# Eight result and twelve token row buffers, eight more slots for late weights, and merges one piece by partition, four tiles later

## The reference, cut to what matters

```
u  = layernorm twice of x;  xz = u @ in_proj.T;  x_in, z = split(xz)          # 256 + 256 features
xc = silu(causal depthwise conv of x_in, 4 taps)
dt, B, C = split(xc @ x_proj.T)                                               # 8, 16, 16
delta = softplus(dt @ dt_w.T + dt_b)
h_t = exp(delta * A) * h_{t-1} + delta * B * xc      # a scan over time, for 256 features x 16 states
y = (sum over states of h * C + xc * D) * silu(z);   x1 = ... + y @ out_w.T
x2 = x1 + (silu(gate) * val) @ ffp.T                  # gate, val from a norm of x1
x3 = x + x2
logits = layernorm(x3) @ Ws + bs;  the two best of 8 experts, weights by softmax
out = x3 + sum over the two experts of weight * (silu(m @ Wg[e]) * (m @ Wu[e])) @ Wd[e]   # 128 -> 344 -> 128
```

## Time and profile before

| what | value |
|---|---|
| median of 3 runs | 918.84 us (916.27 to 920.73) |
| the profiled execution's own time | 916.48 us |
| its span, first to last instruction | 914.6 us |
| mean granted TensorE clock | 0.789 |
| busy: PE, DVE, ACT, POOL | 634.4, 766.2, 447.8, 577.8 us |
| DMA | 126.06 MB, mean 138 GB/s |

### The profile page before, as it was taken

How to read it: one execution, slowest core, us unless ns; L and a number is a source line. 1 busy time by engine, 2 the same in 40 slices (tenths; PEclk the granted TensorE clock), 3 DMA queues, 4 the chain that set the end, 5 groups by cost and what they waited for, 6 DMA issues and landing times.

```text
span 914.6 us, 12461 instructions
## 1 busy us (share of the span) xinstructions
PE 634.4 (69%) x3482; PEld 488.9 (53%) x3482; DVE 766.2 (84%) x1158; ACT 447.8 (49%) x924; POOL 577.8 (63%) x488
## 2 busy tenths in 40 slices
PE   4357377478757785797589658865884686887874
PEld 1134354365346435684477337743773475777863
DVE  1389899999989989989999999999999996363453
ACT  2446455644654475545555564647553352333421
POOL 1096376458746995789668976898589845235422
PEclk9577578758656966997699768977796679799987
DMA  6734233333323346533553355335543553446694
GB/s 175 244 104 142 91 116 100 120 94 121 124 76 96 118 117 169 161 113 99 175 161 107 96 185 151 127 93 161 172 120 113 149 145 94 125 140 191 185 308 132
DMA packets 99767, 126.06 MB, mean 138 GB/s; under 512 B 11831, under 2 KB 63875, under 8 KB 99683
## 3 DMA queue, kind: packets, MB, share of 16 engines
q1 hardware_dynamic: 95155, 115.89, 42.7%
q0 software_dynamic: 4544, 9.38, 2.8%
HBM read 113.23 MB, written 16.34 MB: 142 GB/s over the span
## 4 chain that ended last, share of the span: by engine, by line
DVE 35%; PE 29%; issue 18%; ACT 7%; DMA 4%; SPq 3%; POOL 3%; DVEq 1%; another core or an unknown queue 0%; POOLq 0%; ACTq 0%
DVE state L908 19%; DVE product L916 4%; PE work_front L1062 4%; PE y L1104 3%; PE gate L1181 3%; PE work_front L1068 3%; PE up L1188 3%; PE up L1199 2%; DVE stats L841 2%; PE work_front L1076 1%; DVE silu_m L1027 1%; PE work_side L1142 1%; DMA y_dram<-y_rows,x_rows 1%; DVE x_tok L945 1%; DVE conv L882 1%
## 5 line engine op out<-in xcount | busy, mean ns | idle before, releaser
L670 POOL TENSOR_TENSOR inflow<-du,b_wide 128x1024 f32<-128x1024 f32 x128 | 308.9, 2416 | 191.6 <-DVE product L916 153.8
L775 ACT ACTIVATE decay<-delta,a_neg 128x512 f32<-128x512 f32 x256 | 174.0, 689 | 199.4 <-DVE state L908 191.5
L1104 PE MATMUL y<-ident,product 128*128 128x128 f32 x1024 | 181.8, 337 | 119.9 <-DVE product L916 119.9
L1104 PEld LDWEIGHTS y<-ident,product 128*128 128x128 f32 x1024 | 153.5, 177 | 172.9 <-DVE product L916 138.3
L908 DVE TENSOR_TENSOR_SCAN state<-decay,carry,inflow 128x512 f32<-128x512 f32 x192 | 235.2, 1266 | 0.8 <-ACT decay L775 0.8
L916 DVE TENSOR_TENSOR product<-state,c_wide 128x1024 f32<-128x1024 f32 x128 | 189.5, 1480 | 1.3
L697 POOL DMA_INDIRECT y_dram<-y_rows,x_rows x78 | 87.5, 1121 | 90.5 <-ACT y_rows L831 82.4
L691 POOL DMA_INDIRECT row_dram<-m_tok,place x64 | 71.8, 1122 | 22.1 <-issue 12.8
L908 DVE TENSOR_TENSOR_SCAN state<-decay,inflow 128x512 f32<-128x512 f32 x64 | 74.5, 1205 | 7.0 <-ACT decay L775 4.5
L1062 PE MATMUL work_front<-u_t,w_tap 128*128 128x512 f32 x128 | 63.0, 618 | 4.0 <-ACT u_t L725 1.7
L1181 PE MATMUL gate<-x_cols,w_stage 128*128 128x128 f32 x306 | 50.5, 309 | 7.4 <-ACT x_cols L821 6.9
(11 more groups left out here) (199 smaller groups left out, 1118.4 us busy)
## 6 DMA issues: line engine op xcount, KB each, us to landing
b_wide<-bc_dram SPq DMA_DIRECT2D x128, 256.0 KB
c_wide<-bc_dram SPq DMA_DIRECT2D x128, 256.0 KB
w_stage<-gate_up_dram SPq DMA_DIRECT2D x78, 344.0 KB
x_rows<-row_dram SPq DMA_DIRECT2D x78, 65.0 KB
x_tok<-in_x SPq DMA_DIRECT2D x8, 256.0 KB, 6.0
out<-x_tok SPq DMA_DIRECT2D x8, 256.0 KB
inflow<-y_dram SPq DMA_DIRECT2D x6, 256.0 KB, 4.8
gate_up_dram<-in_Wg SPq DMA_DIRECT2D x1, 1376.0 KB, 9.1
```

The source lines that it names most:

```text
L670: e.tensor_tensor(inflow[:, key % 3], du[:, c % 2], b_wide[:, key % ROW_SLOTS:key % ROW_SLOTS + 1, :].to_broadcast([P, HALVES, CHUNK]), AL ...
L775: e.activation(decay_bank[h][:], delta[:, c % 2, h, :], ACT.Exp, scale=a_neg[:, h, n:n + 1]).then_inc(S["decay"], 1)
L1104: t = e.matmul(y_bank[s // 2][:, y_at(s, h)], product[:, key % 2, h, s * P:(s + 1) * P], ident[:], is_transpose=True, start=False, stop=n ...
```

## The change

- `X_SLOTS` goes from 8 to 12, `Y_SLOTS` from 4 to 8. The wait of `load_x` (L620) is not edited: for a job from 12 on it waits on the semaphore of slot `key % 8` for `(key - 12) // 8 + 1` landings.
- Behind the scan, weights also go to eight more slots, in `xc`, `silu_z`, `delta`, `conv` and `tanh_c`. A load takes the first free slot; `load_w` has its own loop ahead of the row loads, over the next 13 jobs in the tail. The first load into such a slot waits for the last `y_gate`.
- The numbers in `tag` and the view `y_chunks` change, so that a partition's results of a chunk (two experts, four tokens) lie in one run of 4 KB; `fetch_y` is one DMA of 512 KB.
- Fetches of chunks 0 to 6 stand at steps 0, 1, 3, 4, 6, 7 and 9 behind the first; a merge comes four steps behind its fetch, a store five.
- Semaphores: the merge waits on the chunk's `d_x`, four start semaphores become one.

```
-X_SLOTS = 8
-Y_SLOTS = 4
+LATE_SLOTS = 8
+X_SLOTS = 12
+Y_SLOTS = 8
...
+    def load_w(m):
+
+        if m < len(JOBS) and JOBS[m][0] in listed and ("load_w", m) not in done:
+            for q in range(W_SLOTS + (LATE_SLOTS if late else 0)):
+                users = [t for t, (slot, _, _) in w_slot.items() if slot == q]
+                if not users or ("up", users[-1]) in done:
+                    w_slot[m] = q, len(users), users[-1] if users else None
+                    put("load_w", m)
+                    return
...
-            if (m < W_SLOTS or ("up", m - W_SLOTS) in done) and JOBS[m][0] in listed and ("load_w", m) not in done:
-                put("load_w", m)
+            load_w(m)
...
-                for at in range(len(span) + 3):
-                    merges.append([(step, span[at - lag]) for step, lag in (("fetch_y", 0), ("merge", 2), ("store", 3)) if 0 <= at - lag < len(span)])
+                at = {c: k + k // 2 for k, c in enumerate(span)}
+                for now in range(at[span[-1]] + MERGE_LAG + 2):
+                    merges.append([(step, c) for step, lag in (("fetch_y", 0), ("merge", MERGE_LAG), ("store", MERGE_LAG + 1)) for c in span if at[c] + lag == now])
...
+    late.append(last)
     for t in range(m, len(JOBS) + 2):
...
+        for q in range(t, t + W_SLOTS + LATE_SLOTS):
+            load_w(q)
         for q in range(t, t + X_SLOTS):
             load(q, 0)
...
-        y_chunks = y_dram[0:TOPK * TOKENS, :].rearrange("(q c s p) d -> c p q s d", q=TOPK, s=SUB, p=P)
+        y_chunks = y_dram[0:TOPK * TOKENS, :].rearrange("(c p q s) d -> c p q s d", q=TOPK, s=SUB, p=P)
...
-                    for q in range(TOPK):
-                        e.dma_start(y_back[key][:, q], y_chunks[key][:, q]).then_inc(S[f"d_merge{key}"], 16)
+                    e.dma_start(y_back[key], y_chunks[key]).then_inc(S[f"d_x{key}"], 16)
...
-                    if key >= W_SLOTS:
-                        e.wait_ge(S["up"], key - W_SLOTS + 1)
+                    if ahead is not None:
+                        e.wait_ge(S["up"], ahead + 1)
+                    elif q >= W_SLOTS:
+                        e.wait_ge(S["y_gate"], 2 * CHUNKS)
```

More of the change, by code:

```diff
@@ L121 @@
 BACK_BEFORE_ROUND = 6
+MERGE_LAG = 4
 def plan():
@@ L178, in first_half @@
             put("up", m)
-    sent, listed, loaded = set(), set(), {}
+    sent, listed, loaded, w_slot, late = set(), set(), {}, {}, []
     def queue_back(c):
@@ L313, in plan @@
         put(step, last)
-    return order, tail
+    return order, tail, w_slot
 def mamba_moe_block(nc, T, out):
@@ L417, in mamba_moe_block @@
                   for part in (inflow[:, 0], inflow[:, 1], inflow[:, 2], product[:, 0], product[:, 1], state[:, 0], state[:, 1], du[:, 0])]
+        late_parts = [xc[:, 0], xc[:, 1], silu_z[:, 0], silu_z[:, 1], delta[:, 0], delta[:, 1], conv, tanh_c]
+        late_parts = [part.rearrange("p h t -> p (h t)")[:, 0:2 * FF_WIDE].rearrange("p (j f) -> p j f", j=2) for part in late_parts]
+        w_slots = [w_stage[:, q] for q in range(W_SLOTS)] + late_parts
         var_one = sb("var_one", [P, SUB])
@@ L431, in mamba_moe_block @@
         gate_bank, up_bank = bank("gate"), bank("up")
-        order, tail = plan()
+        order, tail, w_slot = plan()
         banks = [(gate_bank, up_bank), tuple(decay_bank), tuple(y_bank)]
@@ L439, in mamba_moe_block @@
             + [f"d_b{q}" for q in range(ROW_SLOTS)] + [f"d_c{q}" for q in range(ROW_SLOTS)]
-            + [f"d_rows{q}" for q in range(X_SLOTS)] + [f"d_w{q}" for q in range(W_SLOTS)] + [f"d_scatter{c}" for c in range(CHUNKS)]
-            + ["d_gate_up", "d_pads", "bases", "tag0", "tag1", "list", "listed_count", "merged"] + [f"d_y{q}" for q in range(Y_SLOTS)] + [f"d_merge{c}" for c in range(CHUNKS)]
-            + ["halved", "a_exp", "a_neg", "diag", "minus_half", "ones", "ser_shift", "w_tap", "back_halved", "halo"]
+            + [f"d_rows{q}" for q in range(X_SLOTS)] + [f"d_w{q}" for q in range(W_SLOTS + LATE_SLOTS)] + [f"d_scatter{c}" for c in range(CHUNKS)]
+            + ["d_gate_up", "d_pads", "bases", "tag0", "tag1", "list", "listed_count", "merged"] + [f"d_y{q}" for q in range(Y_SLOTS)]
+            + ["halved", "a_exp", "a_neg", "diag", "constants", "w_tap", "back_halved", "halo"]
             + ["stats0", "aggr0", "stats2", "aggr2", "stats3", "aggr3", "rstd0", "rstd2", "rstd3", "shift0", "shift2", "shift3"]
@@ L449, in mamba_moe_block @@
             + ["rank", "count", "place"]
-            + ["x_turn", "x_cols", "w_pad", "gate", "up", "tanh_m", "silu_m", "moe_h", "down", "y_rows"])}
+            + ["x_turn", "x_cols", "gate", "up", "tanh_m", "silu_m", "moe_h", "down", "y_rows"])}
         x_dram = T["x"].rearrange("b (c s p) d -> (b c) p s d", s=SUB, p=P)
@@ L597, in _ @@
                     k, j = JOBS[key]
-                    q = key % W_SLOTS
+                    q, use, ahead = w_slot[key]
                     if j == 0:
@@ L626, in _ @@
         def _(e):
-            e.memset(minus_half[:], -0.5).then_inc(S["minus_half"], 1)
-            e.memset(ser_shift[:], LOG1P_SHIFT).then_inc(S["ser_shift"], 1)
-            e.memset(ones[:], 1.0).then_inc(S["ones"], 1)
-            e.memset(w_stage[:, :, :, FF:], 0.0).then_inc(S["w_pad"], 1)
+            e.memset(minus_half[:], -0.5).then_inc(S["constants"], 1)
+            e.memset(ser_shift[:], LOG1P_SHIFT).then_inc(S["constants"], 1)
+            e.memset(ones[:], 1.0).then_inc(S["constants"], 1)
+            e.memset(w_stage[:, :, :, FF:], 0.0).then_inc(S["constants"], 1)
             e.memset(left[:, :, 0:4], 0.0).then_inc(S["bases"], 1)
@@ L1016, in _ @@
                 elif name == "merge":
-                    e.wait_ge(S[f"d_merge{key}"], 16 * TOPK)
+                    e.wait_ge(S[f"d_x{key}"], 16 * 2)
                     for q in range(TOPK):
@@ L1176, in _ @@
                     e.wait_ge(S["x_cols"], key + 1)
-                    e.wait_ge(S[f"d_w{key % W_SLOTS}"], 16 * (key // W_SLOTS + 1))
+                    slot, use, _ = w_slot[key]
+                    e.wait_ge(S[f"d_w{slot}"], 16 * (use + 1))
                     if key == 0:
-                        e.wait_ge(S["w_pad"], 1)
+                        e.wait_ge(S["constants"], 4)
                     for q in range(NF):
-                        t = e.matmul(gate[:, q * P:(q + 1) * P], w_stage[:, key % W_SLOTS, 0, q * P:(q + 1) * P], x_cols[:, key % 2, :], start=True, stop=True)
+                        t = e.matmul(gate[:, q * P:(q + 1) * P], w_slots[slot][:, 0, q * P:(q + 1) * P], x_cols[:, key % 2, :], start=True, stop=True)
                     t.then_inc(S["gate"], 1)
@@ L1187, in _ @@
                     for q in range(NF):
-                        t = e.matmul(up[:, q * P:(q + 1) * P], w_stage[:, key % W_SLOTS, 1, q * P:(q + 1) * P], x_cols[:, key % 2, :], start=True, stop=True)
+                        t = e.matmul(up[:, q * P:(q + 1) * P], w_slots[w_slot[key][0]][:, 1, q * P:(q + 1) * P], x_cols[:, key % 2, :], start=True, stop=True)
                     t.then_inc(S["up"], 1)
```

10 lines of the change are left out of this document (5 added, 5 removed).

## The result

The changed kernel took 925.64 us (median of 20 runs, 918.67 to 931.91); the kernel before, measured beside it, 918.23 us (20 runs, 914.34 to 922.30). The ratio is 1.0074, interval [1.0052, 1.0096]: slower by 0.7%. I had forecast 914.0 us and given "slower" a chance of 0.11. Two later measurements on other chips, each beside runs of the kernel before, gave 0.9998 [0.9969, 1.0027] and 1.0033 [0.9996, 1.0069]. So the sign is settled in one direction only: in no measurement is the change faster, and it costs 0 to 0.7% by the chip or the session. The expected 4.7 us are missing everywhere, and that is the question here.

The account below looks back on a forecast made before the run. DVE was taken to bound the scan; in the tail PE, then merges with DMA share 0.97 and about 12 us of waits. +3.5 - 0.8 - 6.0 - 1.4 = -4.7 us, 914.1 on the median; forecast 914.0, range 905 to 921.

Parts of the forecast that it names:

- The scan: Scan stage: extra row buffers and slot rule change no place in the list, DVE hides semaphore waits; 0, ±1 us.
- Result buffers: Result buffers 4 to 8: ScalarE's long waits are late signals from PE and stay; 0, lower bound -8.3 us.
- The rival that gave 906: Result buffers did bind, so eight remove the four stalls and fetches perhaps come in time: -13 us, 906; chance 0.17.
- Row buffers: Row buffers 8 to 12: rows up to job 59 go ahead of round 7's pads, -0.8 us; a loss in the merges.
- the exact wait: Rival without waits for adds 68 and 69: fetch 1 sooner, fetch 0 not; 0.4 us, inside the range, no own chance.
- The start of round 6: Tail, step 38: ten weight loads ahead of row load 41 delay job 42; +3.5 us, ends +2 and +5.5.
- the second figure: Start of round 6: rows stand behind 3.52 MB of weights in flight, landing at 782.4, +4.6 us; without that, +2.9.
- The merges: Merge stretch: merge 0 waits 5.6 us, merge 1 0.4, later fetches in time; -6.0 us, good end -12.
- the bad end of the range: Merge stretch: landings of 5 us each push fetch 0 and fetch 1, about 899; with a further clock drop 0.
- The end: Behind job 77: adds no longer queue, -1.0; last fetch one issue, -0.4; together -1.4 us, ends -2.4 and 0.
- The gain of the merges is given back: SP's blocked row loads delay fetches 0 and 1, merges give -2, clock's saving fails: 0, 919; chance 0.24.
- The slower rival: Round 6: rows of jobs 41 and 42 behind 3.52 MB, drain about 22 us or more; about 927; chance 0.09.

Follow-up runs that it names:

- e6_slotrule: The kernel before with only the changed kernel's slot rule, the lowest-numbered free weight slot: 919.73 us, ratio 0.9977.
- e9_y8: The kernel before with eight result buffers instead of four, nothing else: 921.43 us, ratio 1.0024.
- e11_y4: The changed kernel with four result buffers instead of eight: 918.15 us, ratio 0.9989 to the kernel before.
- before_again: The kernel before, unchanged, profiled once more on the chip of the others: 917.84 us, ratio 1.0018.
- e3_exact: The changed kernel with each row load waiting for the add twelve jobs back: 911.01 us, ratio 0.9933 to the kernel before.
- e2_oldest: The changed kernel with weight loads taking the slot free for longest, not the lowest-numbered: 917.37 us, ratio 0.9985 to the kernel before.
- e4_rowsfirst: The changed kernel with row loads ahead of the loop of weight loads in each tail step: 917.78 us, ratio 1.0002 to the kernel before.
- x_all: The changed kernel with longest-free slot, row wait for the add twelve jobs back, rows ahead of weights: 900.8 us, 0.9820; on a third chip 902.23 us, 0.9828.
- x_lowest: x_all with the lowest-numbered free weight slot again: 906.38 us, ratio 0.9867 to the kernel before.
- x_y4: x_all with four result buffers instead of eight: 906.29 us, ratio 0.9870 to the kernel before.
- e10_x12: The kernel before with twelve row buffers instead of eight, still four result buffers: 916.61 us, ratio 0.9972.
- x_nolate: x_all without the eight late weight slots (LATE_SLOTS = 0): 910.7 us, ratio 0.9893 to the kernel before.

## Why the prediction was wrong, step by step

The sum first. On the profiled executions I forecast -4.7 us and +4.2 came out (918.8 against 914.6). The start came out 3.2 us worse than forecast, the middle 2.3, the merges 2.9, the end 2.0, the scan 1.5 better: 8.9 in all. From 914.0 to 925.64 it is 11.6; the other 2.7 are the median's distance from the profiled execution, 5.0 us here and 2.4 in the kernel before, and I have no cause for them.

- **The scan, 0: no cost shown, wrong in its reason.** I wrote that "the new slot rule change[s] no place in the list" and never worked out which slots it gives. It gives three of five. SP then waits 90 us for `up`, hidden in the scan (e6_slotrule, 0.9977). The last of these waits isn't hidden; see the start of round 6.
- **Result buffers, 0: right.** Four long remote waits of ScalarE stay with eight buffers (e9_y8); in the changed kernel's first trace two are left (7.4 us), and two in `e11_y4` with four buffers. Such waits appear in every profile of three sessions and in none of the three others, whatever the kernel: they belong to the chip or the session. That they come from two kinds of indirect DMA in a row, as I suspected, isn't enough: `before_again` has the same sequence on POOL and none of them. The rival that gave 906 falls.
- **Row buffers: the step that failed.** I saw that the wait is still for the add of `key - 8` where `key` leaves 4 to 7, that the row loads now come four steps earlier, and that SP blocks with other things behind it. Then I priced two consequences of it and not the mechanism. Ahead of the pads of round 7 I took -0.8. That wait did go: PE no longer waits for job 56 (0.84 us before). But the row loads that held SP, and the loads added behind them, put the pads off as well, by 6.7 us counted from job 42, and PE pays at job 63 (6.66 and 5.72 us on the second and third chip). So the middle is 1.5 us longer on the profiled execution, and equal on the second chip. For the exact wait I took 0.4 us. It was worth 8 us in the merges and at least 0.65% in all (e3_exact 0.9933, the change 0.9998 at the least, on different chips, the intervals apart). The error was to compare the new wait with the old kernel's ("as before"): before, the list asked for the rows of a job when its slot was about to come free; now it asks four jobs sooner, so the same wait is entered sooner and held longer (36.4 us, 13.5 at the longest, against 27.0 and 7.3).
- **The start of round 6, +3.5 became +6.7: mechanism right, one wait missing.** The row load goes at 777.70, the time that I had worked out, and that is luck: nine weight loads stand ahead of it and not ten, and the first goes at 769.79 and not at 767.75. PE takes the rows up at 782.74; I had 780.7 without a queue in front and 782.4 with it, and took a value between. The queue counts in full: 343 GB/s while PE stands. By the Trainium skill (DMA: Bandwidth & Descriptors, section "Queues, rings and completion order") each DMA engine takes the descriptors of one issuing engine's ring in ring order, which I had cited for the second figure; the trace agrees, 782.74 against 782.4. Counted on the clock job 42 starts 5.2 us later, inside my bound of 5.5. Counted from the end of the scan it is 6.7, and 7.0 on the second chip, where the scan did not end sooner. The term I had put at nothing is the slot rule: it puts off the pads, and all behind them, by 2.1 us. Without it the start is 24.4 (e2_oldest), with the rows ahead of the weights 21.8 (e4_rowsfirst), with both 21.2 (x_all).
- **The merges, -6.0 became -3.1: one landing.** With job 67 at 873.97 instead of 867.26, fetch 0 should have gone at 874.0 + 6.7 = 880.7; it went at 880.65. Merge 0 should have waited 5.6 us and waited 5.84. Fetch 1 should have gone at 883.7 and went at 885.97. The chain that ended last shows why, in order of time:

```profile
881.50 3.92 DMA y_dram<-y_rows,x_rows
885.97 3.77 DMA inflow<-y_dram
```

The add of job 68 was issued 0.7 us later than I had and took 3.92 us to land instead of the 2.22 that I copied from the last add, which runs with nothing beside it. Merge 1 waited 2.06 and merge 2 0.74, and their late starts (2.4 + 0.7) are the missing 3 us. I had the bad end of the range for it and took the quiet duration.
- **The end, -1.4 became +0.6: mechanism wrong.** I expected the last three adds to queue no longer because DVE would pace the jobs. They queue as before. The `down` of jobs 75 to 77 stand one behind the other at the end of PE's list, whatever paces the jobs ahead:

```profile
903.97 0.93 PE L1219 MATMUL y<-w_down,h_cols 128*128 x6 [0.58 <-issue]
904.74 0.83 PE L1219 MATMUL up<-w_down,h_cols 128*128 x6
905.73 0.93 PE L1219 MATMUL decay<-w_down,h_cols 128*128 x6 [0.16 <-DVE h_cols L1051]
```

```profile
905.58 1.44 POOL L716 DMA_INDIRECT y_dram<-y_rows,x_rows  x1 [1.95 <-ACT y_rows L850]
907.33 0.95 POOL L716 DMA_INDIRECT y_dram<-y_rows,x_rows  x1 [0.30 <-ACT y_rows L850]
908.59 0.96 POOL L716 DMA_INDIRECT y_dram<-y_rows,x_rows  x1 [0.30 <-issue]
```

Three adds, which start at least 1.26 us apart, stand behind three `down` in 1.76 us of starts. The first is also longer, 1.44 us, beside a merge that now falls there (905.51 on DVE). The last fetch in one piece took 3.47 us from issue to landing; the two took 3.66 (906.75 to 907.16 + 3.25): 0.2 us and not 0.4.
- **The rivals.** "The gain of the merges is given back" came nearest in its mechanism, and in its number for the second and third chip (917.49 and 920.59): it gave 919 from -2 in the merges and no gain ahead of the pads, by SP's blocked row loads. It had 0.24. The slower rival's 927 is nearer to the first median, 925.64, but not by its mechanism. That the cost at the start is the drain of the weights was in the slower rival too, but its price (22 us of drain) did not occur; 13 us did (769.79 to 782.74).

What stays open: why the ratio is 1.0074 in the first measurement and 0.9998 and 1.0033 in the others. The remote waits don't settle it, since in the first measurement the kernel before had them too. Where the scan ends differs by up to 8 us between executions of one kernel (754 to 762 us for `x_turn` of job 37), and no experiment here was aimed at that. How much of `x_all` is due to the slot rule is open as well (0.9820 and 0.9828 with it, 0.9867 without, on different chips). Its start differs by 1.4 us (21.2 against 22.6). The longer middle of `x_lowest` (87.5 against 82.1 and 81.1) can't be put to the rule: `x_y4` has the longest-free slot and 87.3. Those two come from sessions with the remote waits, `x_all` from sessions without.

## What to carry to other kernels

A deeper buffer moves its loads forward in the issuing engine's list, and each wait in front of them is then entered sooner and held longer; so work out, for every load, which completion it really waits for, and what stands behind it in that queue. Check index arithmetic against the new sizes: a wait that was exact for 8 over 4 is not for 12 over 8. Ask the same of a rule that picks a free slot: the lowest free one may be the one freed last. Parts of a change can cover for one another, so take them out of it singly as well as adding them singly to the old kernel: here the late weights looked idle from one side and were worth 3.5% from the other.

## What the runs showed of the hardware

- An indirect DMA on POOL that starts inside an addition of a merge on DVE takes longer. The timelines of POOL and DVE in `before_again`:

```profile
876.07 1.48 POOL L697 DMA_INDIRECT y_dram<-y_rows,x_rows  x1 [1.71 <-ACT y_rows L831]
880.39 0.96 POOL L697 DMA_INDIRECT y_dram<-y_rows,x_rows  x1 [2.85 <-ACT y_rows L831]
...
898.98 1.23 POOL L697 DMA_INDIRECT y_dram<-y_rows,x_rows  x1 [1.59 <-ACT y_rows L831]
```

```profile
875.29 1.42 DVE L1021 TENSOR_TENSOR x_tok<-x_tok,inflow 128x512 f32<-128x512 f32 x2 [4.00 <-DMA inflow<-y_dram]
...
879.70 1.42 DVE L1021 TENSOR_TENSOR x_tok<-x_tok,inflow 128x512 f32<-128x512 f32 x2 [1.94 <-DMA inflow<-y_dram]
...
897.96 1.42 DVE L1021 TENSOR_TENSOR x_tok<-x_tok,state 128x512 f32<-128x512 f32 x2 [1.59 <-DMA state<-y_dram]
```

A merge is two additions of 0.7 us. The add at 876.07 starts with 0.64 us of the second to go and is 0.52 us longer than a quiet one (0.96); the one at 898.98 has 0.40 to go and is 0.27 longer; the one at 905.58 in the changed kernel starts 0.07 us into the first and is 0.48 longer. The one at 880.39 starts just where the first addition ends (879.70 + 0.70) and is not longer. The Trainium skill (SBUF — State Buffer, section "SBUF: two separate sides") tells of a port pair that a DVE operation with two inputs in SBUF and a GpSimd operation that reads SBUF take exclusively, whichever starts first, for a whole instruction; the trace agrees, since the surplus follows what is left of the addition, though no run here separates it from other causes.
- The landing of the same 128-row add took 2.21 us with nothing beside it and 3.92 us in the merges.
- The long remote waits behind `down` come and go with the session, not with the kernel; three such waits are 8 to 9.5 us of ScalarE's time (e10_x12 8.0, x_nolate 9.5).
